# Folding an attention gate into the output projection's weights, with a new order of steps in a batch

## The reference, cut to what matters

```python
ga = (2 * (ga >= 0) - 1) * jnp.maximum(jnp.abs(ga), 0.25)      # one row of 256 per batch
h = _layernorm(x, axis=-1) * (1 + ca) + sa
x = x + ga * _L0_attn_ref(h, ...)                              # ends in: out @ w_out.T
h = _layernorm(x, axis=-1) * (1 + cb) + sb
x = x + gb * _L0_ffn_ref(h, ...)
```

## Time and profile before

| | before |
|---|---|
| median of 3 executions | 1072.28 us (1072.27 to 1074.97) |
| profiled execution | 1072.48 us |
| its span, first to last instruction | 1070.4 us |
| busy: PE, DVE, POOL, ACT | 1007.9, 767.8, 413.9, 403.3 us |
| setup, first instruction to batch 0 | 61.6 us |
| the six looped batches | 754.5 us |

### The profile page before, as it was taken

The page is one execution under the profiler, slowest core; times in us unless marked ns, Lnnn a source line. Parts: engine busy times, 40 slices in busy tenths (PEclk is TensorE's granted clock), DMA queues, the critical chain, the costliest instruction groups (busy, mean ns, idle before and its releaser), DMA issues.

```text
span 1070.4 us, 24879 instructions
## 1 busy us (share of the span) xinstructions
PE 1007.9 (94%) x9783; PEld 735.9 (69%) x9783; DVE 767.8 (72%) x1518; ACT 403.3 (38%) x731; POOL 413.9 (39%) x357
## 2 busy tenths in 40 slices
PE   5979989999899999999899998999999998999888
PEld 4656667766686667766677666876768766776566
DVE  6767688586967868677776769768686777866454
ACT  4334533254314443145341643235431444315320
POOL 1526442264405454055432634145540644316200
PEclk9989999999999998999899999999999999999999
DMA  6220000200002000200002000020001000010000
GB/s 195 60 90 2 2 1 1 70 2 2 1 2 70 2 1 1 70 2 2 1 1 71 1 2 1 1 71 1 2 1 43 29 2 1 1 50 2 2 1 20
DMA packets 22232, 23.59 MB, mean 22 GB/s; under 512 B 6314, under 2 KB 20138, under 8 KB 22130
## 3 DMA queue, kind: packets, MB, share of 16 engines
q1 hardware_dynamic: 22130, 22.02, 6.7%
HBM read 17.80 MB, written 4.21 MB: 21 GB/s over the span
## 4 chain that ended last, share of the span: by engine, by line
PE 72%; DVE 11%; issue 8%; POOL 4%; ACT 3%; DMA 1%; POOLq 0%; DVEq 0%; SPq 0%; ACTq 0%
PE ring L1158 15%; PE ring L1006 11%; PE ring L1007 9%; PE ring L1008 9%; PE ring L1235 8%; PE av L1174 7%; PE ring L1130 5%; DVE mcol L888 2%; ACT pt L694 2%; POOL prod L564 2%; DVE xr L927 2%; PE ring L1142 2%; PE av L1187 1%; PE ring L1224 1%; DVE room L908 1%
## 5 line engine op out<-in xcount | busy, mean ns | idle before, releaser
L694 ACT ACTIVATE pt<-ring 128x384 f32<-128x384 f32 (+1 forms) x384 | 170.8, 532 | 316.9 <-PE ring L1158 281.2
L579 POOL TENSOR_SCALAR_AFFINE_SELECT pt<-pt 128x512 f32<-128x512 f32 x128 | 79.5, 637 | 391.9 <-ACT pt L694 391.9
L864 DVE TENSOR_TENSOR prod<-ring,table 128x1024 f32<-128x1024 f32 x128 | 155.5, 1218 | 92.7 <-PE ring L1008 92.1
L888 DVE TENSOR_REDUCE mcol<-ring 128x1 f32<-128x128 f32 (+3 forms) x512 | 211.4, 481 | 12.8 <-PE ring L1135 9.6
L1158 PE MATMUL ring<-rows 32*128 32x512 f32 (+3 forms) x3072 | 177.3, 331 | 10.0 <-ACT pt L694 5.0
L1158 PEld LDWEIGHTS ring<-rows 32*128 32x128 f32 x3072 | 131.6, 184 | 61.6 <-issue 30.0
L570 POOL TENSOR_TENSOR rows<-prod,rows 128x1024 fp32r<-128x1024 f32 x64 | 152.7, 2395 | 34.6 <-ACT rows L674 34.6
L563 POOL TENSOR_TENSOR prod<-prod 128x512 f32<-128x512 f32 x64 | 82.4, 1287 | 134.9 <-DVE prod L864 133.8
L1130 PE MATMUL ring<-rows 32*128 32x256 f32 (+3 forms) x1024 | 78.4, 356 | 21.6 <-ACT cont L686 6.9
L674 ACT ACTIVATE rows<-prod 128x1024 fp32r<-128x1024 f32 x64 | 67.6, 1063 | 58.3 <-PE ring L1158 36.9
L1130 PEld LDWEIGHTS ring<-rows 32*128 32x128 f32 x1024 | 44.5, 185 | 61.9 <-issue 42.2
(11 more groups left out here) (169 smaller groups left out, 1630.6 us busy)
## 6 DMA issues: line engine op xcount, KB each, us to landing
xn<-x_dram SPq DMA_DIRECT2D x8, 512.0 KB, 3.9
xr<-x_dram SPq DMA_DIRECT2D x8, 512.0 KB, 4.2
out_dram<-xr SPq DMA_DIRECT2D x8, 512.0 KB, 3.2
gate_bc<-gates_scratch SPq DMA_DIRECT2D x8, 256.0 KB, 4.8
pt<-wmod_dram SPq DMA_DIRECT2D x1, 1536.0 KB, 6.4
pt<-gup_t_dram SPq DMA_DIRECT2D x16, 96.0 KB, 2.5
dn<-wu_t_dram SPq DMA_DIRECT2D x1, 640.0 KB, 10.0
xr<-wk_t_dram SPq DMA_DIRECT2D x1, 512.0 KB, 8.2
```

The lines of the kernel that those rows point to most:

```text
L694: sc.activation(pt[:, PT_AT[n] + h * w:PT_AT[n] + (h + 1) * w], ps[:, 0:w], ACT.Exp, scale=SCALE).then_inc(exp_ready.sem, 1)
L864: ve.tensor_tensor(prod[:, s % PROD, :, :], ps[:, :].unsqueeze(1).broadcast_to([P, 2, S]), table[:, :, :], ALU.mult).then_inc(rotated.sem, 1)
L888: last = ve.reduce_max(mcol[:, q, h * HR + HD:h * HR + HD + 1], ps[:, at:at + (q + 1) * P], AX_X)
```

## The change

The gate is multiplied into the weights instead of the result: a new step `wofold`, once per batch on POOL, writes `wo_gated = wo * gate` into the first two quarters of `xn`, and `mix` takes its weights from there. `mixed` then only adds the PSUM result to the residual. `wofold` waits for the gate row, for the last `low1` step (from then on `xn` is free until `norm2`), and in batch 0 for the load of `wo`; `mix` waits for `wofold`. Readers that waited for the gating multiply wait for the add. The wait for the split expert weights moves from `loads` to the first `exp`. The body list is written anew; the last list only gains `wofold`, behind `attn_out.03`.

```diff
-load_next.1 loads.0 maxima.010 rope.0200 reduce.010 score.000 rotate.0200 rope.0201 exp.000 rotate.0201 maxima.011
...
+score.000 load_next.1 rope.0200 exp.000 maxima.010 rotate.0200 clear.000 loads.0 rope.0201 reduce.010 score.001
+rotate.0201 value.000 exp.001 maxima.011 clear.001 rope.0210 reduce.011 combine.020 maxima.012 rotate.0210 rope.0211
+reduce.012 score.002 rotate.0211 kcon.02 exp.002 shift.01 qcon.02 shifted.01 kcon_hi.02 clear.002 stats1.1 value.001
+hi.020 value.002 qcon_hi.02 lo.020 score.010 kcon_lo.02 attn_out.00 rope.0300 qcon_lo.02 exp.010 combine.021 score.011
+rotate.0300 hi.021 clear.010 rope.0301 exp.011 maxima.020 rotate.0301 clear.011 value.010 reduce.020 pow1.1 score.012
+lo.021 norm1.1 value.011 exp.012 combine.030 maxima.021 rope.0310 reduce.021 hi.030 clear.012 maxima.022 rotate.0310
+lo.030 kcon.03 reduce.022 rope.0311 kcon_hi.03 qcon.03 rotate.0311 turn1.10 qcon_hi.03 turn1.11 kcon_lo.03 combine.031
+shift.02 modulate1.10 qcon_lo.03 value.012 shifted.02 modulate1.11 score.020 low1.10 attn_out.01 hi.031 score.021
+exp.020 maxima.030 clear.020 exp.021 value.020 reduce.030 clear.021 lo.031 score.022 low1.11 maxima.031 exp.022
+value.021 reduce.031 clear.022 maxima.032 latent.1 reduce.032 rope.1000 latent_hi.1 shift.03 value.022 shifted.03
+latent_lo.1 score.030 rotate.1000 attn_out.02 rope.1001 exp.030 score.031 rotate.1001 clear.030 combine.100 value.030
+exp.031 score.032 clear.031 wofold.0 rope.1010 exp.032 rope.1011 hi.100 rotate.1010 clear.032 value.031 lo.100
+rotate.1011 value.032 rope.1100 attn_out.03 combine.101 values.10 values.11 rotate.1100 mix.00 mix.01 mixed.00 kcon.10
+mixed.01 qcon.10 kcon_hi.10 rope.1101 values_out.10 stats2.0 qcon_hi.10 pow2.0 values_out.11 qcon_lo.10 rope.1110
+hi.101 norm2.0 lo.101 rotate.1101 turn2.00 turn2.01 qcon.11 kcon_lo.10 modulate2.00 combine.110 rotate.1110 rope.1111
+modulate2.01 low2.00 qcon_hi.11 maxima.100 low2.01 qcon_lo.11 gate.00 rotate.1111 gate.01 reduce.100 tanh.00 logits.0
+tanh.01 gated.00 maxima.101 gated.01 logits_copy.0 up.00 reduce.101 maxima.102 turn_l.0 gate.02 turned_l.0 top.0
+gate.03 tanh.02 upped.00 top2.0 ...
...
+weigh.05 down.00 weighed.03 upped.05 weighed.04 weighed.05 down.01 join.00 kcon.11 join.01 kcon_hi.11 store.0
+kcon_lo.11
...
+        wo_gated = xn[:, 0:NPAIR, :]
...
+                    elif kind == "wofold":
+                        if isinstance(b, int) and b == 0:
+                            pool.wait_ge(ld_wo, 16)
+                        wait(pool, gate_loaded, b, ahead, 0)
+                        if part == "last":
+                            wait_alone(pool, lo_ready[1], b, ahead - 1, EC - 1)
+                        else:
+                            wait_alone(pool, lo_ready[0], b, ahead + 1, EC - 1)
+                        pool.tensor_tensor(wo_gated, wo[:, :, :], gate_bc[:, 0:E].unsqueeze(1).broadcast_to([P, NPAIR, E]),
+                                           ALU.mult).then_inc(wo_ready.sem, 1)
...
-                        gate = gate_bc[:, 0:E].unsqueeze(1).broadcast_to([P, 2, E])
-                        ve.tensor_tensor(sum2[:, :, :], ps[:, :].rearrange("p (t e) -> p t e", t=2), gate, ALU.mult)\
-                          .then_inc(mix_gated.sem, 1)
-                        wait(ve, mix_gated, b, ahead, i)
-                        ve.tensor_tensor(xr[:, 2 * i:2 * i + 2, :], xr[:, 2 * i:2 * i + 2, :], sum2[:, :, :], ALU.add)\
-                          .then_inc(mix_added.sem, 1)
+                        ve.tensor_tensor(xr[:, 2 * i:2 * i + 2, :], xr[:, 2 * i:2 * i + 2, :],
+                                         ps[:, :].rearrange("p (t e) -> p t e", t=2), ALU.add).then_inc(mix_added.sem, 1)
...
                         if i == 0:
+                            wait(pe, wo_ready, b, ahead, 0)
                             wait(pe, pair_ready, b, ahead, NPAIR - 1)
...
-                                last = pe.matmul(ps[:, t * E:(t + 1) * E], on[:, pair, tok:tok + P], wo[:, pair, :],
+                                last = pe.matmul(ps[:, t * E:(t + 1) * E], on[:, pair, tok:tok + P], wo_gated[:, pair, :],
```

More of the change, by code:

```diff
@@ new lines @@
+mixed.01 qcon.10 kcon_hi.10 rope.1101 values_out.10 stats2.0 qcon_hi.10 pow2.0 values_out.11 qcon_lo.10 rope.1110
+hi.101 norm2.0 lo.101 rotate.1101 turn2.00 turn2.01 qcon.11 kcon_lo.10 modulate2.00 combine.110 rotate.1110 rope.1111
+modulate2.01 low2.00 qcon_hi.11 maxima.100 low2.01 qcon_lo.11 gate.00 rotate.1111 gate.01 reduce.100 tanh.00 logits.0
+tanh.01 gated.00 maxima.101 gated.01 logits_copy.0 up.00 reduce.101 maxima.102 turn_l.0 gate.02 turned_l.0 top.0
+gate.03 tanh.02 upped.00 reduce.102 up.01 tanh.03 hi.110 gate.04 ex.0 upped.01 lo.110 gated.02 up.02 tanh.04 top2.0
@@ L109 @@
+combine.111 up.03 gated.03 up.04 upped.02 gated.04 turn_w.0 upped.03 shift.10 wT.0 upped.04 gate.05 hi.111 wT_lo.0
+shifted.10 lo.111 weigh.00 tanh.05 weigh.01 weighed.00 weigh.02 weigh.03 weigh.04 gated.05 up.05 weighed.01 weighed.02
+weigh.05 down.00 weighed.03 upped.05 weighed.04 weighed.05 down.01 join.00 kcon.11 join.01 kcon_hi.11 store.0
+kcon_lo.11
 """
@@ L121 @@
 shifted.03 score.030 clear.022 value.022 exp.030 attn_out.02 score.031 clear.030 value.030 exp.031 score.032
-clear.031 exp.032 clear.032 warm.00 value.031 value.032 warm.01 attn_out.03 mix.00 mix.01 warm.02 mixed.00 mixed.01
+clear.031 exp.032 clear.032 warm.00 value.031 value.032 warm.01 attn_out.03 wofold.0 mix.00 mix.01 warm.02 mixed.00 mixed.01
 stats2.0 pow2.0 norm2.0 turn2.00 turn2.01 warm.03 modulate2.00 modulate2.01 low2.00 low2.01 logits.0 logits_copy.0
@@ L287, in block_program @@
         pair_ready = Count(sem("pair_ready"), NPAIR)
[L288 removed]
+        wo_ready = Count(sem("wo_ready"), 1)
         mix_added = Count(sem("mix_added"), 2)
@@ L374, in reader @@
                 "shift": lambda: (shifted, ahead, step[2]),
-                "mix": lambda: (mix_gated, ahead, step[2]),
+                "mix": lambda: (mix_added, ahead, step[2]),
                 "logits": lambda: (logits_copied, ahead, 0),
@@ L637, in program @@
                         sc.activation(gu_hi[:, k, :], gu_st[:, k, :], ACT.Copy).then_inc(ffn_hi_ready, 1)
-                    elif kind == "loads" and part == "body" and isinstance(b, int):
-                        sc.wait_ge(ffn_split, EC)
                     elif kind in ("modulate1", "modulate2"):
@@ L689, in program @@
                         w = ST_W[n]
+                        if isinstance(b, int) and b == 0 and g == 0 and n == 0:
+                            sc.wait_ge(ffn_split, EC)
                         wait(sc, value_added, b, ahead, (g * NST - 1, g * NST - 2, g * NST)[n])
@@ L915, in program @@
                         if i == 0:
-                            wait(ve, gate_loaded, b, ahead, 0)
                             wait(ve, res_loaded, b, ahead, 0)
@@ L1178, in program @@
                         i = step[2]
-                        if isinstance(b, int) and b == 0 and i == 0:
-                            pe.wait_ge(ld_wo, 16)
                         if i == 0:
+                            wait(pe, wo_ready, b, ahead, 0)
                             wait(pe, pair_ready, b, ahead, NPAIR - 1)
@@ L1200, in program @@
                         wait_alone(pe, logits_copied, b, ahead, 0)
-                        wait_alone(pe, mix_gated, b, ahead, 0)
+                        wait_alone(pe, mix_added, b, ahead, 0)
                         for t in range(TT):
```

3 lines of the change are left out of this document (removed).

## The result

The changed kernel takes **1103.7 us** (median of 4 runs, 1100.4 to 1104.0) against 1073.6 for the kernel before (4 runs): a ratio of 1.0285, 95% interval 1.0262 to 1.0308. It is 30 us slower, and 46 us from the forecast of 1058, outside its range. The profiled execution took 1103.95 us, 1102.2 of it span.

The account below looks back on a forecast made before the run. PE, busy 94% of the span, bounds the kernel, so only its idle time and slow stretches can be won. 12.6 + 4.0 + 1.0 - 1.0 = 16.6, less 2.8 allowed, leaves 13.8: 1058 us, range 1046 to 1074.

Parts of the forecast that it names:

- A row against a rule: norm1 and norm2 beside POOL's work: L841's 0.41 us for 256 elements, as bn_stats, taken to mean no delay.
- Rival 4: norm1.1 and norm2 wait for POOL, PE losing 2.6 at maxima.022 and 2.4 at turn2 a batch: 1093 us, chance 0.10.
- The middle: Score and maxima steps mid-batch: waits of 3.25 us for 2.2 in the old order, a loss of 1.05 a batch.
- rival 3: The three exp waits in the middle cost 0.6 us more each: 1071 us, chance 0.14.
- Behind mix: From mix to gate.00: new stalls of 1.45 us for 3.85, a gain of 2.4 a batch.
- the hold of maxima.101: Behind mix, maxima.101 takes 2.65 us for 0.80; this 1.85 us hold was to go.
- The clock: Looped batches: 1.2 GHz stretches, starting within the hold of maxima.101, were to go; 4.0 of 4.5 us gained once.
- mix's wait of 1.0: Ahead of mix: 0.95 us a batch lost in the old order, with 0.05 more lost in the new.
- the joint: Batch start, at maxima.010, rope.0200 and score.000: 0.9 us lost now, 0.2 each left at score.001 and score.002, gain 0.5.
- the last batch: Old list kept: 2.4 us lost at the seam at maxima.010, 1.4 gained at PE's wait for norm2, net loss 1.0.
- the allowance of 0.4: Some thirty bank hand-overs with under 0.3 us of margin: 0.4 us a batch for misses, 2.8 in all.

Follow-up runs that it names:

- e7: The kernel before, with each pass of norm1 and norm2 cut into two of 128 columns: 1076.79 us, one run.
- e3: The changed kernel with POOL's lo.101 held until norm2 is done and lo.021 until the next batch's norm1 is done: 1073.67 us against 1072.94, 1.0003.
- e12: e9 with the changed kernel's whole front up to value.032, and lo.021 held behind norm1: 1050.44 us against 1072.40, 0.9785.
- e9: Fold with old order up to attn_out.03, then the new order with colliding steps moved apart, lo.101 early, no holds: 1043.15 us against 1072.66, 0.9724.
- e4: The kernel before with the fold alone, old order of steps, wofold between clear.031 and clear.032: 1062.66 us against 1072.94, 0.9905.

## Why the prediction was wrong

**The step that failed** is "so I price it at no delay", in "A row against a rule". The price came from L841's duration, 0.41 us for 256 elements like bn_stats' 0.41, which the trace has beside POOL too (212.54 to 213.93, beside the subtraction of 212.50). Equal durations don't make equal paces. e7 shows that two thirds of L841 are a fixed part, and that its columns go twice as fast as a reduction's. The row that was nearest in kind, L835 at 0.44 us beside POOL instead of 0.17, had the answer and was outvoted by a row nearest in size. The rule that the prediction weighed against it (the Trainium skill, "SBUF — State Buffer", section "Who interferes with whom") is the one the trace agrees with: the norm passes went from 407 to 1135 and 853 ns, and back when POOL's work was held off. Its "fully blocks" fits too: the pass ends 0.15 us after POOL's instruction, as if all of its columns were still to do (0.13 us by e7). In place of no delay, norm1.1 ended 3.35 us late and norm2 2.03 in a batch, and holding POOL off them was worth 29.4 us (e3).

**Rival 4**, at a chance of 0.10, is what happened, in its two places. Its delays were priced well: norm1.1 "some 3 us late" (3.35), 2.6 at maxima.022 (2.37 lost there start to start, mean of the looped batches), norm2 2.4 late (2.03), 2.4 at turn2 (2.37 lost there, of which e3 without the collision still loses 0.35). That its sum of 35 us lies near the 29.4 of e3 is partly luck. It had no price for the slow clock behind the two waits, 2.3 us a batch, and none for what the delays hide: with the holds 1.1 us a batch more is lost at score.020 and score.021, and 1.4 ahead of gate.00.

**The middle** was to cost 0.85 + 0.45 + 0.6 for the three steps behind a score, 0.35 for score.020, 3.25 in all. In the changed kernel the start-to-start losses are 0.86 at score.021, 1.05 at maxima.030, 0.83 at maxima.031, 0.19 at score.020, 0.18 at maxima.020 and 0.33 at score.030, together 3.4: the term was sound as it stood. With norm1 cured, in e3, score.021 loses 1.38 and score.020 0.79. That is rival 3's direction, 1.1 us a batch, but up to 0.66 of it is the price of the hold, by hi.031's idle time; e12's 1.3 against the old front carries the same hold.

**Behind mix** the hold of maxima.101 went, the add is 0.69 us, and the fold is hidden: all as forecast. What was mis-sized were two more meetings of DVE and POOL on SBUF. low2 beside combine.110 was 0.5 at gate.00; it is 1.64 of start-to-start loss in e3, though only 0.25 in the changed kernel. top2's L963 and L967 were not priced: weigh.00 and maxima.102 together had 0.45, and weigh.00 alone loses 1.37. The kernel before has such a meeting, at a place where PE doesn't wait: its L942, a 128x128 step of top.0 with both operands in SBUF, takes 1.4 us beside POOL's work in seven batches and 0.29 alone in the last. The timeline of the kernel after shows top2's two steps, DVE and then POOL, beside combine.111 (its first half here):

```profile
696.29 1.25 DVE L963 SCALAR_TENSOR_TENSOR room<-room 128x128 f32<-128x128 f32 x1
697.58 1.27 DVE L967 TENSOR_TENSOR room<-room,small 128x128 f32<-128x128 f32 x1
...
696.11 1.29 POOL L564 TENSOR_TENSOR prod<-prod 128x512 f32<-128x512 f32 x1
```

The first stands beside combine.111's first half, the second beside its second half (L565, from 697.36 to 698.70); in the old order they took 0.26 and 0.29 us, and they do again in e9, where combine.111 stands ahead of top2.

**The clock** term, 4.0 us, rested on the waits being gone. Stretches at the 1.2 GHz level came back instead, behind the norms' waits: against e3, kcon.03 to qcon.03 take 1.5 us a batch longer and turn2.00 to rope.1111 0.8. In e3 and e9, without those waits, the looped batches run at a clock of 1.00, so this term fell with the first.

**Right:** the fold at 1.30 us; mix's wait of 1.0; the joint, near enough (0.45 lost ahead of score.000 and 0.23 at score.002, where 0.2 each was forecast at score.001 and score.002); the last batch. There maxima.010 waits 2.51 us at the seam (forecast 2.4), and turn2 0.83 instead of 2.14, a gain of 1.3 (forecast 1.4):

```profile
981.15 0.74 PE L1136 MATMUL ring<-rows 32*128 32x512 f32 x8 [2.51 <-DVE cont L881]
...
1062.11 1.09 PE L1073 MATMUL ring<-ident,xn 128*128 128x128 f32 x8 [0.83 <-DVE xn L852]
```

**The sum** closes for the changed kernel. A looped batch took 130.8 us (784.58 / 6), 7.2 over the forecast's 123.6 (125.0 less 1.8, plus the allowance of 0.4). Over their prices lie maxima.022 by 2.4, turn2 by 1.9, the slow clock by 2.3 and weigh.00 by 0.9, together 7.5; what is left is small and nearly cancels. So nearly all of it hangs on norm1.1, norm2 and top2 beside POOL.

**What stays open.** What the new middle costs when norm1 is free and POOL is not held was not run. Why e4's gain is 10 us and not 15 was seen at maxima.101 but not tried by an edit of its own.
